# Two decoder layers on one core: VectorE's waits for its own results moved to the next piece, and every order of pieces laid out anew

## The reference, cut to what matters

```python
x = x + _L0_attn_ref(layernorm(x), ...)         # 16 heads of 16, 4 kv heads, rms norm, rope, tanh cap 50, causal softmax
x = x + _L0_xattn_ref(layernorm(x), ctx, ...)   # 16 heads of 64, scores over ctx, causal, softmax
x = x + _L0_ffn_ref(layernorm(x), ...)          # W1, gelu, W2, 1024 wide, plus outer-product terms m1, m2 from 16 tokens
x = x + _L1_attn_ref(layernorm(x), ...)         # 8 heads of 128, keys and values through a latent of 32, causal softmax
x = x + _L1_xattn_ref(layernorm(x), ctx, mask)  # 16 heads of 16, masked softmax over ctx
x = x + _L1_ffn_ref(layernorm(x), ...)          # gate picks 2 of 4 experts per batch; an expert is an encoder layer
                                                # (self-attention, relu feed-forward of 1024, two layernorms)
```

## Time and profile before

| | us |
|---|---|
| median of 3 timed runs | 3494.66 (3492.86 to 3495.1) |
| the profiled execution, its own time | 3503.45 |
| its span from the first to the last instruction | 3501.8 |
| mean granted TensorE clock | 0.946 of full speed |
| phase 1, about 30 to 945 us | 915, 8 rounds |
| phase 2, about 945 to 2385 us | 1440, 8 rounds |
| phase 3, about 2405 to 3501.8 us | 1096.8, 16 rounds |

### The profile page before, as it was taken

One profiled execution on the slowest core, in us unless ns is written; L12 is line 12 of the kernel. 1 busy time (PEld: TensorE's weight loads), 2 busy tenths in 40 slices (PEclk: granted clock), 3 DMA queues, 4 the chain that ended last, 5 costly groups with the idle time before them and its releaser, 6 DMA issues. The chain is left out here.

```text
span 3501.8 us, 82019 instructions
## 1 busy us (share of the span) xinstructions
PE 3102.8 (89%) x31511; PEld 2454.7 (70%) x31511; DVE 2074.8 (59%) x6892; ACT 1896.8 (54%) x6465; POOL 379.3 (11%) x457
## 2 busy tenths in 40 slices
PE   6999999999787979797979797975899988999997
PEld 5777787777665757575757575754788877878886
DVE  3666566666536363636464646463667766767775
ACT  2655556555433444444444443444667766767775
POOL 1112111122000100000000010000111111111111
PEclk8999999999997989899989998996999999999999
DMA  3000000000110101000001000005001022020000
GB/s 112 16 15 13 12 15 15 16 13 19 39 42 3 31 11 29 12 28 13 28 12 27 13 27 13 11 7 190 16 16 17 15 59 59 15 60 16 15 15 9
DMA packets 63966, 95.74 MB, mean 27 GB/s; under 512 B 7218, under 2 KB 59010, under 8 KB 62034
## 3 DMA queue, kind: packets, MB, share of 16 engines
q1 hardware_dynamic: 55202, 82.74, 7.5%
q0 software_dynamic: 8368, 7.70, 1.9%
HBM read 72.04 MB, written 18.37 MB: 26 GB/s over the span
## 5 line engine op out<-in xcount | busy, mean ns | idle before, releaser
L1545 PE MATMUL bps<-BXT,Bwexp 128*128 128x112 f32 x3072 | 375.3, 280 | 2.3 <-DMA Bwexp<-in_we 0.9
L1545 PEld LDWEIGHTS bps<-BXT,Bwexp 128*128 128x128 f32 x3072 | 364.7, 195 | 17.8 <-issue 6.1
L1658 ACT ACTIVATE BPT<-bps,Blow 112x112 f32<-112x112 f32 x1024 | 349.0, 403 | 43.5 <-DVE Blow L1775 43.5
L1309 DVE CUSTOM_DVE_ANT_0 PON<-pps,PMR 112x375 f32<-112x375 f32 x512 | 260.3, 546 | 120.9 <-PE pps L1053 116.8
L1188 ACT ACTIVATE PPT<-pps,mcol 125x896 f32<-125x896 f32 x192 | 184.7, 1003 | 158.1 <-PE pps L1074 158.1
L1658 ACT ACTIVATION_READ_ACCUMULATOR BPT<-bps,Blow 112x1 f32 x1024 | 258.0, 257 | 0.0
L1623 PE MATMUL bps<-Bwexp,BPT 128*112 128x256 f32 x1024 | 245.6, 384 | 9.0 <-ACT BPT L1682 8.9
L760 POOL TENSOR_TENSOR rstd<-var,nhalf 112x1 f32<-112x1 f32 (+1 forms) x96 | 149.8, 1563 | 748.4 <-DVE var L659 537.2
L1053 PE MATMUL pps<-PKT,PQM 32*112 32x375 f32 x1024 | 134.0, 600 | 89.9 <-DVE Pmx L1309 89.4
L1343 POOL TENSOR_TENSOR Prstd<-Pvar,nhalf 112x1 f32<-112x1 f32 x128 | 72.6, 567 | 1295.8 <-DVE Pvar L1223 1295.8
L1623 PEld LDWEIGHTS bps<-Bwexp,BPT 128*112 128x112 f32 x1024 | 172.8, 177 | 52.3 <-ACT BPT L1682 16.8
(11 more groups left out here) (306 smaller groups left out, 7036.1 us busy)
## 6 DMA issues: line engine op xcount, KB each, us to landing
Bwexp<-in_we SPq DMA_DIRECT2D x7, 2311.0 KB, 23.8
PCX<-in_ctx SPq DMA_DIRECT2D x24, 375.0 KB
out<-BY POOLq DMA_DIRECT2D x64, 112.0 KB, 3.0
BXIN<-xmid SPq DMA_DIRECT2D x61, 112.0 KB, 2.0
Bwexp<-in_we SPq DMA_DIRECT2D x7, 770.0 KB, 5.4
Brexp<-in_re SPq DMA_DIRECT2D x7, 672.0 KB, 10.5
XIN<-in_x SPq DMA_DIRECT2D x32, 112.0 KB
CX<-in_ctx SPq DMA_DIRECT2D x32, 112.0 KB
```

The lines of the kernel that those rows point to most:

```text
L1309: m = v.tensor_tensor_reduce(out=ON[s][0:T, i * LC:(i + 1) * LC], in0=bank[s][i][0:T, 0:LC], in1=MR[s][:, :], scale=1.0, scalar=-3.0e38, o ...
L1545: m = mm(o[:, j * T:(j + 1) * T], wt[:, c, n0 + j * 128:n0 + (j + 1) * 128], rhs[:, c, :], start=(c == 0), stop=(c == 1))
L1658: m = A(PT[s][0:T, h, :], bank[s][i][0:T, v * T:(v + 1) * T], ACT.Exp, scale=0.25, bias=low[s][:, h:h + 1], accum_out=sums[s][:, h:h + 1])
```

## The change

1. All 15 strings of `ORDER` are replaced by others of the same length: the same pieces in another order, on all five engines.
2. VectorE's wait for its own result moves from the end of a piece to the begin of the same lane's next piece: in phase 1 behind the addition at line 718, in phase 2 behind the one at line 1296 and behind seven of the eight r steps (line 1313), in phase 3 behind the normalisation at line 1787 and the addition at line 1791. The wait for `m_in` moves from the end of `QM` to r0.

The instructions, their operands and the number of waits stay as they are.

```diff
@@ -57,97 +57,97 @@
 ORDER = {
-    "act2": ("333130203030113133320203211010101012201220102201210312332232010101010101031201302130213230201312"
...
+    "act2": ("323322301222332323223233001120130120132300213100101101001120312323232323232323201012301201303120"
...
-    "dve2": ("332331100211002233030112021010120103102310120133012013201201320132013232323232320100110011001313"
...
+    "dve2": ("332233220011001122332323230101223323230231230231023123230201310101010101010101201232332233223301"
...
-    "pe2": ("333313013021202033001313133200322110101010122012010122200121023123001130130123201323010122012301"
...
+    "pe2": ("332233223031022122332323223230312302310011201013232030212313002310123123010123230230123012312003"
...
-    "pe3": ("321032312102300123013231321301230133331211132132232201201212023000230032303230201323333201222310"
...
+    "pe3": ("321032130212300123013231321321302333232232302310202121023101023100312313010302013233233201223212"
...
@@ -715,9 +715,11 @@
 
                     yield
                     normalise(X)
-                    chained(v.tensor_tensor(X[s][:, :], X[s][:, :], row[:, :], ALU.add))
+                    v.tensor_tensor(X[s][:, :], X[s][:, :], row[:, :], ALU.add).then_inc(vec_done[s], 1)
                     for g in range(2):
                         yield
+                        if g == 0:
+                            t.wait(vec_done[s])
                         t.wait(xf_psum[s])
                         v.scalar_tensor_tensor(out=QT[s][:, 4 * g:4 * g + 4, :], in0=bank[s][g][:, 0:QW].rearrange("p (c q) -> p c q", c=4),
                                                scalar=0.125, in1=bq8[:, 4 * g:4 * g + 4].unsqueeze(2).to_broadcast((128, 4, T)),
@@ -1293,23 +1295,27 @@
 
                     yield
                     normalise(X)
-                    chained(v.tensor_tensor(X[s][:, :], X[s][:, :], ybo, ALU.add))
-                    yield
+                    v.tensor_tensor(X[s][:, :], X[s][:, :], ybo, ALU.add).then_inc(vec_done[s], 1)
+                    yield
+                    t.wait(vec_done[s])
                     t.wait(la_psum[s], 2)
                     for c in range(C2):
                         m = v.scalar_tensor_tensor(out=QM[s][:, c, :, :], in0=b0[:, c * T:(c + 1) * T].unsqueeze(1).to_broadcast((128, 2, T)),
                                                    scalar=bfold[:, 8 + c:9 + c], in1=hm2, op0=ALU.add, op1=ALU.mult)
                     m.then_inc(la_ready[s], 1)
-                    t.wait(m_in[s], 16)
                     for r in range(8):
                         yield
+                        if r:
+                            t.wait(mx_ready[s])
+                        else:
+                            t.wait(m_in[s], 16)
                         t.wait(s_psum[s])
                         for i in range(2):
                             h = 4 * (2 * half(s, r // 4) + i) + r % 4
                             m = v.tensor_tensor_reduce(out=ON[s][0:T, i * LC:(i + 1) * LC], in0=bank[s][i][0:T, 0:LC], in1=MR[s][:, :], scale=1.0,
                                                        scalar=-3.0e38, op0=ALU.add, op1=ALU.max, accum_out=mx[s][:, h:h + 1])
                         m.then_inc(mx_ready[s], 1)
-                        t.wait(mx_ready[s])
+                    t.wait(mx_ready[s])
                     m3 = mx[s][:, :].rearrange("p (g k) -> p g k", g=4)
                     high, low = [MXB[s][:, :].rearrange("p (g n k) -> p g n k", g=4, k=4)[:, :, n, :] for n in range(2)]
                     chained(v.tensor_copy(high, m3))
@@ -1785,11 +1791,12 @@
                     layernorm()
                     yield
                     normalise(ZN).then_inc(xn_ready[s], 1)
+                    yield
                     t.wait(xn_ready[s])
-                    yield
                     scale_shift(ZN, "n1w", "n1b")
-                    chained(v.tensor_tensor(Z[s][:, :], Z[s][:, :], rr(s, "l2b"), ALU.add))
-                    yield
+                    v.tensor_tensor(Z[s][:, :], Z[s][:, :], rr(s, "l2b"), ALU.add).then_inc(vec_done[s], 1)
+                    yield
+                    t.wait(vec_done[s])
                     t.wait(y_psum[s])
                     chained(v.tensor_tensor(X[s][:, :], Z[s][:, :], b0[0:T, 0:D], ALU.add))
                     layernorm()
```

More of the change, by code:

```diff
@@ L76 @@
[L76 to L90, removed]
@@ L99 @@
[L99 to L105, removed]
@@ new lines @@
+    "act3": ("321032130210321032313213210231033222330302212103210032312313010023213302212310310310202121032100"
+            "323123130100232133022123103103102021210321003231231301002321330221231031031020212103210032312313"
+            "010023213302212310310310202121032100323123130100232133022123103103102021210321003231231301002321"
+            "330221231031031020212103210032312313010023213302212310310310202121032100323123130100232133022123"
+            "103103102021210321003231231301002321330221231031031020212103210032312313010023213302212310310310"
+            "202121032100323123130100232133022123103103102021210321003231231301002321330221231031031020212103"
+            "210032312313010023213302212310310310202121032100323123130100232133022123103103212020130211003231"
+            "23130100223130321202101010110100"),
@@ new lines @@
+    "dve1": ("321433221332232324010011300132203021332230301321203201021310030210123133013023323223122102002011"
+            "001103113221301233223030132120320102131003021012313301302332322312210200201100110311322130123322"
+            "303013212032010213100302101231330130233232231221020020110011031132213012332230301321203201021310"
+            "030210123133013023323223122102002011001103113221301233223030132120320102131003021012313301302332"
+            "322312210200201100110311322130123322303013212032010213100302101231330130233232231221020020110011"
+            "031132213012332230301321203201021310030210123133013023323223122102002011001103113221301233223030"
+            "1321203201021310030210123101021011"),
@@ new lines @@
+    "pool1": ("321320103201332201013201332201013201332201013201332201013201332201013201332201013201332201013201"),
+    "pool2": ("332200112301230123223301203011012301232233012030110123012322330120301101230123223301203011012301"
+            "2322330120301101230123223301203011012301232233012030110123012301"),
+    "pool3": ("323321201100323322101100323322101100323322101100323322101100323322101100323322101100323322101100"
+            "323322101100323322101100323322101100323322101100323322101100323322101100323322101100323322101100"),
@@ new lines @@
+    "sp1": ("320132013332220001113201333222000111320133322200011132013332220001113201333222000111320133322200"
+            "01113201333322220000111133220011"),
+    "sp2": ("230123012232233301012010130122322333010120101301223223330101201013012232233301012010130122322333"
+            "0101201013012232233301012010130122322233330101010011223233010101"),
+    "sp3": ("321032103333222211011000333322221101100033332222110110003333222211011000333322221101100033332222"
+            "110110003333222211011000333322221101100033332222110110003333222211011000333322221101100033332222"
+            "1101100033332222110110003333222211011000333322221101100033221100"),
```

126 lines of the change are left out of this document (61 added, 65 removed).

## The result

The changed kernel takes 3388.89 us (median of 4 runs, 3380.12 to 3394.1) against 3494.88 us (4 runs): a ratio of 0.9693, interval 0.9669 to 0.9716. Where the time went is read from the two profiled executions: 3503.45 us before and 3394.1 us after, 109.4 us apart.

A forecast was written before the change was run, and what follows sets the result against it. TensorE's own work bounds phases 1 and 3, a TensorE-VectorE loop a stretch of phase 2. Terms -16, -16, -12 and -5 gave -49 us, cut to -37: 3458 us by the timed runs, own range 3430 to 3485, whole range 3410 to 3507.

The forecast's parts named there:

- The waits: VectorE's moved waits: 0.12 us each, 1.7 us a round or 13 us in phase 2, nothing in phases 1 and 3.
- Phase 2's round, -2.0: Phase 2's new orders, waits included: 2.0 us a round gained, -16 us in 8 rounds (bounds -48, +37).
- that is 4.6 longer, against 6.7 moved out: Phase 2: stretch from leader's r0 to follower's st0 grows from 62.4 to 67.0 us, taking in 6.7 us of TensorE work.
- nearly no gap: Phase 2's round until 1591 us, ahead of the leader's r steps: TensorE was read as having nearly no gap.
- The heads, -5: Starts of phases 2 and 3: first lanes run in the order their data is loaded, -5 us (bounds -10, +5).
- the transfer bounds the start anyway: Heads: a weight transfer of 19.02 us begins phase 3's chain and limits what the lane order can gain.
- Phase 3's round, -0.8: Phase 3: feed-forward halves behind the next scores cover half of 1.6 us of exponential waits, -12 us in 15 rounds.
- The rivals' lost microsecond for lane 0's input step: Phase 3: late input step and regrouped pieces add 1.25 us a round or more; about 3503 us, chance 0.06.
- Phase 1's round, -2.0: Phase 1: five projections cover the attention-times-value piece's wait for VectorE's causal mask, 2.0 us a round, -16 us.
- Three quarters: Whole kernel: the summed gain of -49 us cut to -37 for new stalls that a hand sum misses.
- Rival 3: Phase 2: follower's r block late, moved matmuls delay the leader's r steps; 4.6 us a round lost, 3507 us, chance 0.13.
- rival 4: Phase 2: a quarter of 23.7 us idle closes, -6 us a round; 3420 us or less in all, chance 0.12.

The follow-up runs named there:

- the exchanged kernels: Changed kernel and kernel before, each with lanes 0 and 2, 1 and 3 exchanged in all phase 2 strings: 3402.6 us and 3508.18 us.
- The kernel with the pieces ahead of r0: Changed kernel with the following pair's v01, tXN2 and both la on TensorE moved back ahead of the leader's r0: 3451.5 us, 0.9863.

## Why the prediction was wrong in size

The direction was right, and so were parts of the mechanism; the terms were too small, the heads and phase 3 above all, and the sum was then cut.

- **The waits, 13 us in phase 2, nothing in phases 1 and 3.** The price was right: with the waits moved, the four instructions of two lanes' r steps start 0.47 us apart throughout, where the earlier trace rows has 0.59.

```profile
1540.05 0.55 DVE L1315 CUSTOM_DVE_ANT_0 PON<-pps,PMR 112x375 f32<-112x375 f32 x1
...
1540.52 0.54 DVE L1315 CUSTOM_DVE_ANT_0 PON<-pps,PMR 112x375 f32<-112x375 f32 x1
...
1540.99 0.54 DVE L1315 CUSTOM_DVE_ANT_0 PON<-pps,PMR 112x375 f32<-112x375 f32 x1
```

  The sum was about right (10 us with the new orders), which is luck, for the place was wrong. In phase 2 ScalarE's 3.34 us a step hid the 0.12 with the old orders, by the trace; in phase 3 I called them covered because TensorE is 95% busy, and each costs 0.10. A busy share does not tell whether a chain through VectorE sets the order in which TensorE can go on. The Trainium skill (VectorE: DVE Perf Modes, section The DRAIN you can't avoid) says that a semaphore after each operation costs nothing extra. The 0.47 us against 0.59, and the 0.40 us a round of four waits, do not agree.
- **Phase 2's round, -2.0, measured -3.9.** The step that failed is "that is 4.6 longer, against 6.7 moved out". The stretch came out at 68.5 instead of 67.0: on the mean of the rounds the leader's r0 to its st0 takes 35.5 us (estimated 34.2), to the follower's r0 4.7 (2.5), and to its st0 28.2 (30.3). That is 1.5 worse. But the rest fell by 8.9 us in these two rounds (9.6 on the mean), not 6.7: 6.6 are TensorE's busy time, as forecast, and 2.3 are idle time where I saw "nearly no gap"; its window had 110.90 - 105.85 = 5.05 us, of which 2.76 are left. TensorE's timeline has the points of that reading:

```profile
1527.02 0.90 PE L1055 MATMUL pps<-PKT,PQM 32*112 32x375 f32 x8
...
1542.16 1.61 PE L1055 MATMUL pps<-PKT,PQM 32*112 32x375 f32 x8 [2.77 <-DVE Pmx L1315]
...
1561.86 0.68 PE L1070 MATMUL pps<-PMXT,msel 32*125 32x112 bf16 x16
...
1567.19 1.61 PE L1055 MATMUL pps<-PKT,PQM 32*112 32x375 f32 x8 [1.06 <-DVE PQM L1303]
```

  The 2.77 us gap stands where VectorE runs the maximum of the other pair's latent attention (line 1282), as 4.72 did in the earlier trace rows. The old order on VectorE had both lanes' maxima ahead of the r step (1593.73 to 1597.24, 3.5 us), the new one has one of them (1538.26 to 1540.05, 1.8 us).
- **The heads, -5, measured -41.** The largest miss. The step that failed is "the transfer bounds the start anyway": the one row behind it is of phase 3, whose start indeed did not move (30.1 us in both). Phase 2's head gave 28.0 of the 41. By the runs 8.6 of them are the same matmuls as in the steady round, which I counted for the rounds and not for the head; the order of the lanes, the reason that I gave, is some 4 by the exchanged kernels (28.0 less 23.8). Phase 1's 10.4 I did not work out at all: TensorE is busy for 4.4 us less there and idle for 6.0 less (windows from 0 to 183.4 and to 173.0 us), and no run here tells the cause.
- **Phase 3's round, -0.8, measured -1.9.** 0.8 of it are the waits; the orders are 63.80 to 62.67, 1.1 us. I halved a gain of 1.6 for stalls that would come; TensorE's waits went from 3.2 to 2.2 us, and the rest is busy time that fell. The rivals' lost microsecond for lane 0's input step did not come. Fifteen times 1.9 is 28.5 of the 34.6 us; the other 6 come from the rounds in which experts change, to which I gave nothing.
- **Phase 1's round, -2.0, measured -1.9.** Right in size by luck, for the reason given is not borne out by the runs. The mask's wait is gone from the round after, but others are there, 3.0 us in all:

```profile
PE ps L396 <- DVE ON L708: 1.4, 2, 0.7
PE ps L482 <- ACT OT L540: 1.4, 2, 0.9
PE ps L456 <- issue: 0.2, 1, 0.2
```

  and filling that stall in the old layout gained nothing. What shortened the round is the layout as a whole; which part of it stays open.
- **Three quarters.** I cut the sum for stalls that no reading sees. Single moves do bring such stalls: of the five kernels that moved single pieces in the hope of a gain none gained, and three lost 10 to 26 us. The three that put pieces of the change back lost 48 to 131 us, more than forecast each time. A whole order laid out anew on all engines did not bring them.

Rival 3, slower since the follower starts late, was wrong in its price and right in half of its mechanism: the follower's r0 does come 4.7 us after st0, and without the matmuls inside the r block the new order loses 3.4 us a round. Its other half, that these matmuls delay the leader's r steps, did not come: from the leader's r0 to its st0 it is 35.5 us where it was 35.3. The time itself is rival 4's (3420 or less), but not its reason: it wanted 6 us a round of phase 2, and 3.9 came.

## What to carry to other kernels

A piece moved on one engine is priced by where it goes and by the orders of its partners: the same 6.7 us of matmuls were free inside one stretch and cost 7.1 in the next, and a projection moved alone waited 2.1 us for a copy that its partner's order had later. So work out the stretch that receives the piece and the stretch that gives it up, each with its own idle time, and the head before the first round like a round. A wait removed from a loop counts only if no other loop through the same engine is slower; look for that other loop's period first. Busy shares say which engine has most work, not which short waits lie on the path.

## What the runs showed of the hardware

In phase 2 a gap on TensorE costs more than its length. After the 2.77 us before 1542.16 the r step took 1.61 us, where the one at 1527.02 takes 0.90; TensorE had worked for 0.90 of the 4 us before 1542, and from there to 1550 the granted clock is 0.50, the 1.2 GHz level. The changed kernel pays for this no more than the old one: 151.5 and 151.3 us of busy time a round. The kernel with the pieces ahead of r0 does. Its six rounds, beside the two rows above:

```profile
1199.52:2264.60 1065.08, 936.15 (x10297) 690.90 (x10297) 546.22 (x2208) 467.58 (x1224) 76.46 (x120) 0.90 0.06 18
```

The same 10297 matmuls take 936.15 us there at a mean granted clock of 0.90, against 908.95 at 0.93. Of the 7.3 us by which its round is longer than the changed kernel's on this mean, 4.5 are busy time and 2.8 idle time.
